# Four-layer graph network: attention products of the middle layers moved to PSUM and scanned two heads at a time

## What is computed

```python
xs = (h @ Ws).reshape(N, H, C)                  # H = 4 heads of C = 32
xd = (h @ Wd).reshape(N, H, C)
e = leaky_relu(sum(xs * a_s)[src] + sum(xd * a_d)[dst], 0.2)   # one score per edge and head
ex = exp(e - segment_max(e, dst)[dst])
alpha = ex / (segment_sum(ex, dst)[dst] + EPS)
out = segment_sum(xs[src] * alpha[:, :, None], dst) + bias
```

## Time and profile before

| | us |
|---|---|
| median of 3 runs | 10716.57 |
| lowest, highest | 10702.52, 10762.04 |
| the profiled execution's own time | 10696.98 |
| its span in the trace | 10695.3 |
| POOL busy | 7165.4 |
| DVE busy | 5556.2 |
| PE busy (matmul) | 4520.8 |
| ACT busy | 2086.2 |

### The profile page before, as it was taken

One profiled execution on the slowest core, in us unless ns is written; L12 is line 12 of the kernel. 1 busy time (PEld: TensorE's weight loads), 2 busy tenths in 40 slices (PEclk: granted clock), 3 DMA queues, 4 the chain that ended last, 5 costly groups with the idle time before them and its releaser, 6 DMA issues. The chain is left out here.

```text
span 10695.3 us, 86620 instructions
## 1 busy us (share of the span) xinstructions
PE 4520.8 (42%) x16860; PEld 2720.4 (25%) x16860; DVE 5556.2 (52%) x10266; ACT 2086.2 (20%) x4254; POOL 7165.4 (67%) x5805
## 2 busy tenths in 40 slices
PE   6388887211111200001000003888888885433332
PEld 5133333211110200001000001444444443333332
DVE  6399998644444344443444444555565544444443
ACT  1211111211111211112111112333333331000002
POOL 2466666488887688886888884555555526888885
PEclk8688888555555555555555556999999985555555
DMA  2433334322223222223222223333333313444445
GB/s 67 122 59 59 59 59 54 87 42 42 42 41 39 45 42 42 42 43 44 43 42 43 42 42 73 90 87 87 88 93 85 89 32 31 36 36 36 36 36 95
DMA packets 775295, 608.14 MB, mean 57 GB/s; under 512 B 441381, under 2 KB 661028, under 8 KB 774068
## 3 DMA queue, kind: packets, MB, share of 16 engines
q0 software_dynamic: 325728, 497.67, 26.0%
q1 hardware_dynamic: 449492, 109.67, 4.9%
HBM read 479.64 MB, written 127.21 MB: 57 GB/s over the span
## 5 line engine op out<-in xcount | busy, mean ns | idle before, releaser
L1640 POOL DMA_INDIRECT big<-table_layer,idx_L x2688 | 3528.8, 1313 | 952.3 <-issue 818.9
L2311 POOL DMA_INDIRECT sums_by_source<-msg,to x896 | 1420.4, 1585 | 286.9 <-issue 241.2
L1651 PE MATMUL own_ps_L<-of_tile_L,big 50*128 50x4 f32 x1344 | 313.1, 354 | 2694.4 <-DVE of_tile_L L1700 2694.4
L936 POOL DMA_INDIRECT big<-table_layer,idx_L x912 | 948.7, 1040 | 517.3 <-issue 299.0
L1710 DVE TENSOR_TENSOR z_L<-own_ps_L,big 128x64 f32<-128x64 f32 x168 | 43.9, 261 | 2034.5 <-DMA big<-table_layer,idx_L 2034.5
L1861 POOL DMA_INDIRECT big<-table_layer,from x900 | 861.1, 957 | 274.3 <-issue 274.3
L1651 PEld LDWEIGHTS own_ps_L<-of_tile_L,big 50*128 50x128 f32 x1344 | 298.6, 325 | 2712.2 <-DVE of_tile_L L1700 2704.7
L1911 PE MATMUL ps<-big,w 128*128 128x512 f32 x1792 | 829.6, 606 | 0.0
L1740 DVE TENSOR_TENSOR_SCAN big<-h 128x2244 f32<-128x2244 f32 x168 | 811.9, 4833 | 15.2
L999 PE MATMUL sums_L<-h,ident 128*128 128x512 f32 x1344 | 723.1, 688 | 169.6 <-issue 132.9
L1998 DVE TENSOR_REDUCE partial<-big 128x128 f32<-128x512 f32 x448 | 462.1, 1041 | 552.0 <-ACT big L1945 494.7
(11 more groups left out here) (411 smaller groups left out, 8962.7 us busy)
## 6 DMA issues: line engine op xcount, KB each, us to landing
big<-table_layer,idx_L POOLq DMA_INDIRECT x3600
table_layer<-xr SPq DMA_DIRECT2D x49, 298.0 KB
big<-table_layer,from POOLq DMA_INDIRECT x900
sums_by_source<-msg,to POOLq DMA_INDIRECT x896
sums_by_source<-big SPq DMA_DIRECT2D x4, 3200.0 KB
q<-sums_by_source SPq DMA_DIRECT2D x28, 448.0 KB, 6.2
own_L<-own_parts_layer SPq DMA_DIRECT2D x232, 40.0 KB
table_layer<-st_L SPq DMA_DIRECT2D x98, 66.0 KB
```

Source lines behind the costliest of these rows:

```text
L936: G.indirect_dma_start(out=g[b][:, u, s, :], out_offset=None, in_=table, in_offset=bass.IndirectOffsetOnAxis(ap=at, axis=0)).then_inc(gath ...
L1640: G.indirect_dma_start(out=ring[b][:, s, :], out_offset=None, in_=tab1_d[l], in_offset=bass.IndirectOffsetOnAxis(ap=idx[b][:, s:s + 1].bit ...
L1651: last = PE.matmul(own_ps[b % 2][:, c * B:(c + 1) * B], own1T[:, c * P:(c + 1) * P], of_tile[b % 2][:, :], start=True, stop=True)
L2311: G.indirect_dma_start(out=sum_d[s], out_offset=bass.IndirectOffsetOnAxis(ap=to[u][:, s:s + 1], axis=0), in_=msg[u][:, s, :], in_offset=No ...
```

## The change

The products and the weights move from SBUF to PSUM. `products_` is a PSUM tile of three banks; its first 1122 words hold the products of two heads at a time, and its last 64 words the weights `wt` of all four heads, which ACT now writes there. `sums` runs twice over its steps, once for each pair of heads: it copies the carried sums, copies the pair's weights into the rows that are scanned with the products, multiplies two heads, and scans 1122 elements. `shrink` and `tot` stay in SBUF. The product's inputs were two SBUF tiles and are now a PSUM and an SBUF tile; so are the scan's.

`own_ps` is left with one bank, so PE now also waits for `args` of the batch before it overwrites it. ACT's wait counts one more, since `args` starts at 1.

```diff
-            shrink, prod = (hf[:, v * WIDE:(v + 1) * WIDE].rearrange("p (a s) -> p a s", s=SLOTS + 1) for v in range(2))
+            shrink = hf[:, 0:WIDE].rearrange("p (a s) -> p a s", s=SLOTS + 1)
...
-                    own_ps = [pb(f"own_ps_{tag}{v}", [P, 512], fp32, ph) for v in range(2)]
+                    prod_ps = pb(f"products_{tag}", [P, 3 * 512], fp32, ph)
+                    prod = prod_ps[:, 0:WIDE // 2].rearrange("p (a s) -> p a s", s=SLOTS + 1)
+                    wt = prod_ps[:, 1472:1472 + H * SLOTS].rearrange("p (h s) -> p h s", h=H)
+                    own_ps = pb(f"own_ps_{tag}", [P, 512], fp32, ph)
...
                                 pe.wait_ge(oh_ok, i * NB + b + 1)
+                                pe.wait_ge(args, i * NB + b + 1)
...
-                            act.wait_ge(args, k + 1)
-                            A.activation(prod[:, :, :].rearrange("p (h c) s -> p h c s", h=H)[:, :, C, 1:SLOTS + 1],
-                                         z[:, :, :], ACT.Exp)
+                            act.wait_ge(args, k + 2)
+                            A.activation(wt, z[:, :, :], ACT.Exp)
...
-                            p4 = prod[:, :, :].rearrange("p (h c) s -> p h c s", h=H)
-                            V.tensor_copy(prod[:, :, 0], tot[1 - b % 2][:, :, SLOTS])
-                            for c in range(H):
-                                last = V.tensor_tensor(p4[:, c, 0:C, 1:SLOTS + 1],
-                                                       bc(p4[:, c, C, 1:SLOTS + 1], 1, C),
-                                                       ring[b][:, :, c * C:(c + 1) * C].rearrange("p s c -> p c s"),
-                                                       ALU.mult)
-                            last.then_inc(used[b], 1)
-                            dve.drain()
-                            dve.wait_ge(kept, k + 1)
-                            V.tensor_tensor_scan(flat(tot[b % 2]), flat(shrink[:, :, :]), flat(prod[:, :, :]), 0.0,
-                                                 ALU.mult, ALU.add).then_inc(scanned, 1)
+                            p4 = prod[:, :, :].rearrange("p (h c) s -> p h c s", c=C + 1)
+                            half = H // 2
+                            for f in range(2):
+                                rows = slice(f * half * (C + 1), (f + 1) * half * (C + 1))
+                                V.tensor_copy(prod[:, :, 0], tot[1 - b % 2][:, rows, SLOTS])
+                                V.tensor_copy(p4[:, :, C, 1:SLOTS + 1], wt[:, f * half:(f + 1) * half, :])
+                                for c in range(half):
+                                    hd = f * half + c
+                                    last = V.tensor_tensor(p4[:, c, 0:C, 1:SLOTS + 1], bc(wt[:, hd, :], 1, C),
+                                                           ring[b][:, :, hd * C:(hd + 1) * C].rearrange("p s c -> p c s"),
+                                                           ALU.mult)
+                                if f:
+                                    last.then_inc(used[b], 1)
+                                dve.drain()
+                                if f == 0:
+                                    dve.wait_ge(kept, k + 1)
+                                last = V.tensor_tensor_scan(flat(tot[b % 2][:, rows, :]), flat(shrink[:, rows, :]), flat(prod[:, :, :]),
+                                                            0.0, ALU.mult, ALU.add)
+                                dve.drain()
+                            last.then_inc(scanned, 1)
...
                         dve.sem_inc(kept, 2)
+                        dve.sem_inc(args, 1)
```

More of the change, by code:

```diff
@@ L1649, in turn @@
                                 pe.wait_ge(oh_ok, i * NB + b + 1)
+                                pe.wait_ge(args, i * NB + b + 1)
                                 for c in range(H):
-                                    last = PE.matmul(own_ps[b % 2][:, c * B:(c + 1) * B], own1T[:, c * P:(c + 1) * P],
+                                    last = PE.matmul(own_ps[:, c * B:(c + 1) * B], own1T[:, c * P:(c + 1) * P],
                                                      of_tile[b % 2][:, :], start=True, stop=True)
@@ L1710, in scores @@
                             V.tensor_tensor(z[:, :, :].rearrange("p h (u s) -> p h u s", s=S),
-                                            bc(own_ps[b % 2][:, 0:H * B].rearrange("p (h u) -> p h u", h=H), 3, S),
+                                            bc(own_ps[:, 0:H * B].rearrange("p (h u) -> p h u", h=H), 3, S),
                                             ring[b][:, :, D:A1].rearrange("p (u s) h -> p h u s", s=S), ALU.add)
```

## The result

| | before | after | ratio (95%) |
|---|---|---|---|
| time, median, us | 10715.24 | 10414.22 | 0.9717 (0.9698 to 0.9737) |
| lowest to highest | 10702.52 to 10762.04 | 10380.19 to 10428.84 | |

The account below looks back on a forecast made before the run. POOL's gather issue was taken as the bound. Of 969.8 us freed, 31 for one-hots and 3.5 at layer ends were deducted: 935 off 10697 gives 9762, about 9775 as median of runs; range 9715 to 9900.

Parts of the forecast that it names:

- What bounds the kernel: Middle layers: POOL's issuing of gathers sets the period, 25.9 us a batch; DVE idles 12.1 us, ACT 10.0.
- Where POOL's extra time came from, and that PSUM lets it go: Middle-layer gathers: 969.8 us extra beside DVE's scan and products with two SBUF inputs; all goes with one in PSUM.
- Rival 4: Middle layers: nothing moves, long gathers have another cause that goes with the scan; 1313 ns mean, 10720, chance 0.03.
- One-hots: First middle layer: DVE's one-hots from two SBUF inputs still hold gathers; 31 us come back, bounds 0 and 92.
- DVE's `sums`: Middle layers: the split and copies add 1.15 us a batch to 9.1, hidden except 3.5 us at layer ends.
- Rivals 3 and 5: Dear PSUM operands in `sums`: 3, half again, ACT's loop bounds, 10025, chance 0.09; 5, twice, some 10785, chance 0.03.
- PE's new wait: Middle layers: `own_ps` comes some 2 us behind L1710; what waits for it is 20 us later, so nothing.
- The step that failed: Middle layers: ACT's loop, bound for 15.8 us a batch, keeps 3.2 us idle, so POOL's 20.1 us sets the period.
- the sum: Whole execution: 969.8 - 31 - 3.5 = 935 us saved.
- the gathers' mean: Middle layers: L1640's gathers fall from a mean of 1313 ns to near 963.
- The sentence on what would make the prediction wrong as a whole: Middle layers: wrong if POOL's start-to-start of 1.257 us is stretched when nothing holds it, for instance by filling DMA queues.

Follow-up runs that it names:

- experiment 3: Eight more ACT drains before each batch's stores: added to the changed kernel 10520.68 us, ratio 0.9842; added to the kernel before 10702.27 us, ratio 0.9995.
- Experiments 1: The changed kernel with products and weights back in SBUF, the split kept: 10569.55 us, ratio 0.9888 to the kernel before (chip 15).
- experiment 4: The kernel before with its products in five PSUM banks, no split: 9300.26 us on chip 3, 9300.33 on chip 0, 10403.54 on chip 7.
- chip 0: The changed kernel run again, unaltered, on another chip than the result's: 9295.38 us, ratio 0.9088 to the kernel before on that chip.
- the split's two traces: The changed kernel with products and weights back in SBUF, on two chips: 10569.55 us (chip 15) and 10104.88 us (chip 0).
- experiment 2: The changed kernel with ACT making the next batch's weights before storing this batch's sums: 10290.16 us, ratio 0.9627 (chip 15); 9303.61 us, 0.9099 (chip 4).

## Why the prediction was wrong

**What bounds the kernel**: right. POOL's issuing set the period before, and eight steps more on ACT cost nothing there (experiment 3).

**Where POOL's extra time came from, and that PSUM lets it go**: right, in size too. Experiments 1 and 4 show the cause: two inputs from SBUF hold POOL with short scans as with long ones, and one input in PSUM lets it go with long scans as with short ones (960 ns mean in experiment 4's kernel). The rule of the Trainium skill ("SBUF — State Buffer", Who interferes with whom), that at most one SBUF input does not contend, agrees: 962 ns mean. Its inference that tensor_tensor with two SBUF inputs does not stall descriptor generation is contradicted by the gathers of 1.31 and 1.65 us beside the products; the scan, which it does not name, held one for 5.53. Rival 4 rested on it and is out.

**One-hots**: 31 us expected, and 2584.6 - 2688 x 0.952 = 25.6 in the trace. One of them, beside L1759:

```profile
2408.15 1.23 DVE L1759 TENSOR_TENSOR big<-big 128x2048 bf16<-128x2048 bf16 x1 [0.32 <-issue]
2408.56 1.63 POOL L1643 DMA_INDIRECT big<-table_layer,idx_L  x1 [0.30 <-issue]
```

**DVE's `sums`**: scans took 2.49 us against 2.50 forecast, products 1.05 against 1.06. On chip 0 it ran from 3009.28 to 3019.07, 9.8 us, where 9.1 + 1.15 had been forecast. Rivals 3 and 5 needed PSUM operands that are dear, and these were not. PE's new wait cost nothing (experiment 4 has none, and the same time).

**The step that failed**: "ACT is nearer: ... it is bound for 15.8 us, and its idle of 10.0 falls to 10.0 - 5.6 - 1.15 = 3.2". The 15.8 us were taken with ACT's stores as they stood while DVE held POOL for 5.6 us in each batch. On chip 0 this was right: ACT idles 2.77 and DVE 2.92 and 5.35, where 3.2 and 5.3 were forecast, and the sum holds (930 against 935). On the chip of the result the stores grew from 3.8 to as much as 15.5 us once POOL was free, because steps of ACT's sequencer slowed, and some of SP's and DVE's. The period did not fall to 20.1: the middle layers took 4179 us for 168 batches, 24.9 with the layers' ends, against 4509 before and 3575 on chip 0. The difference of the last two, 933, is what was due; it takes the kernel before to be as long there on either kind of chip, which no trace of it shows, but the split's two traces do for that kernel (4381 and 4387). Of the 933, 603 were lost. POOL's idle time before its gathers, 1539.0 us against 960.3 on chip 0, holds 579 of them: 582.4 against 141.9 for positions, 956.6 against 818.4 at "issue". It is the outcome of rival 3, ACT's loop as the bound, by another mechanism than it named. That the sum came out within 5 us on chip 0 is no luck of cancelling terms: the gathers' mean, the one-hots and the idle times each came out near their forecast.

The sentence on what would make the prediction wrong as a whole looked at POOL's own start-to-start. That stayed 1.257 us; the others' steps stretched. The warning was in the trace of the kernel before: in the MLP stage, whose gathers I used to show that a PSUM operand releases POOL, SP's steps already took up to 723 ns and POOL waited 603.8 us for positions. I read the gathers of that stage, not what waited beside them.

**Open.** What ACT, SP and DVE share that slows their steps, and what distinguishes the chips. Each chip was used in one spell only, so that it is the chip and not the hour is likely (spells of both kinds alternated) but not shown. On chip 0 ACT's check never took over 18 ns, even in 1125 us of gathers without a break. That the slow steps cause the loss rests on the timeline, the table and experiment 2, which took DVE's chain from behind them and won; no run removed them by themselves.

## What to carry to other kernels

Put one of the two inputs of a large DVE instruction into PSUM when GpSimd issues indirect DMAs beside it: 5.6 us of GpSimd's time a batch came back here, and the scans and products took DVE no longer. Before counting on it, look at a stage of the same trace where nothing holds GpSimd: the other engines' slow steps were to be seen there before the change (up to 723 ns). A loop that has slack on its compute engines can still be bound by register steps. Put what others wait for (here the weights) ahead of work with many of them; it won 124 us where steps were slow and nothing where they were not. And measure on more than one chip.

## What the runs showed that I had not expected

- Register, load and check steps of ACT that have a median of 18 to 284 ns took about 0.70 and up to 1.4 us on two chips (and on that of the result), and SP and DVE had such steps too, while gathers were issued with nothing that held them. POOL kept its 1.257 us from gather to gather. In the result's trace the steps of the first store behind ACT's wait were spared (1 slow in 843).
- The same kernel differed by 4.6% between chips (10,226 and some 10,700 us), and the two kinds disagree on a change: 9% on one, 3% on the other. The granted clock does not tell them apart: the changed kernel's middle layers had 0.50 to 0.51 on both.
- A drain on GpSimd behind 16 indirect gathers cost 3.46 us of a batch of 20.1.
